# Four gate selects moved to GpSimd, softmax sums fetched as sixteen rows, and all engine orders rewritten, in a two-layer attention and LoRA-mixture kernel

## The reference

```
for attn in (a, b):
    x = x + attn(layernorm(x))          # 32 query heads, 8 key/value heads of 16, RoPE, causal softmax
    x = x + ffn(layernorm(x))
ffn(x): gate = x @ gate_w.T             # 8 experts
        two largest, softmax over the two -> w_full (8 weights, 6 of them zero)
        x @ base_w.T + base_b + 2 * sum_e w_full[e] * (x @ lora_A[e].T) @ lora_B[e].T
```

## Time and profile before

| | us |
|---|---|
| median of 3 runs | 813.37 |
| lowest, highest | 803.45, 813.75 |
| the profiled execution | 808.43 |
| its span, first to last instruction | 806.6 |
| TensorE busy | 737.9 |
| VectorE busy | 578.8 |
| GpSimd busy | 566.0 |
| ScalarE busy | 491.5 |

### The profile page before, as it was taken

How to read it: one execution, slowest core, us unless ns; L and a number is a source line. 1 busy time by engine, 2 the same in 40 slices (tenths; PEclk the granted TensorE clock), 3 DMA queues, 4 the chain that set the end, 5 groups by cost and what they waited for, 6 DMA issues and landing times.

```text
span 806.6 us, 15131 instructions
## 1 busy us (share of the span) xinstructions
PE 737.9 (91%) x4340; PEld 562.3 (70%) x4340; DVE 578.8 (72%) x2771; ACT 491.5 (61%) x1086; POOL 566.0 (70%) x669
## 2 busy tenths in 40 slices
PE   7579999999999988989998999999989999989966
PEld 6458467778777765777776787777768677756645
DVE  5587768696878959578684968778585977768333
ACT  5545666575766756567665666766565676566512
POOL 4574787768595967959688695958768596875501
PEclk9778899999999999999999999999999999999888
DMA  9623434545325265352436434253444425342010
GB/s 321 165 75 81 107 88 112 132 111 133 93 92 135 78 161 154 95 122 90 117 98 165 117 109 117 91 122 92 127 109 126 102 84 113 98 109 85 24 49 27
DMA packets 52957, 89.31 MB, mean 111 GB/s; under 512 B 16389, under 2 KB 21253, under 8 KB 52873
## 3 DMA queue, kind: packets, MB, share of 16 engines
q1 hardware_dynamic: 50568, 87.29, 40.8%
q10 hardware_dynamic: 2304, 1.05, 0.5%
HBM read 24.34 MB, written 9.44 MB: 42 GB/s over the span
## 4 chain that ended last, share of the span: by engine, by line
PE 36%; POOL 19%; DMA 19%; DVE 9%; issue 6%; ACT 5%; SPq 4%; ACTq 1%; POOLq 0%; DVEq 0%
DMA QK<-R 7%; DMA ND<-sums 6%; PE SB L444 6%; DVE tw L1031 4%; PE T L460 4%; PE SA L423 3%; POOL R L205 3%; POOL ND L230 3%; POOL PT L1130 3%; PE T L402 2%; PE SA L427 2%; POOL Qs L199 2%; PE T L403 2%; PE T L404 2%; DVE SA L968 2%
## 5 line engine op out<-in xcount | busy, mean ns | idle before, releaser
L968 DVE CUSTOM_DVE_ANT_0 SA<-SA,mask 128x128 f32<-128x128 f32 (+1 forms) x1024 | 333.6, 385 | 59.1 <-PE SA L427 46.1
L764 ACT ACTIVATE PT<-SB 128x512 f32<-128x512 f32 x384 | 218.0, 594 | 80.9 <-PE SB L444 75.8
L1130 POOL TENSOR_SCALAR_AFFINE_SELECT PT<-PT 128x512 f32<-128x512 f32 x256 | 160.3, 634 | 70.6 <-ACT PT L764 68.9
L444 PE MATMUL SB<-QK 100*128 100x512 f32 x384 | 161.5, 438 | 10.7 <-DMA QK<-mT 5.5
L968 DVE DVE_READ_ACCUMULATOR2_ANT nm<- 128x1 f32 x1024 | 141.3, 138 | 0.0
L423 PE MATMUL SA<-QK 96*128 96x512 f32 x256 | 109.2, 428 | 9.9 <-DVE nm L968 8.7
L402 PE MATMUL T<-XH,WQh 128*128 128x256 f32 x384 | 112.1, 292 | 5.0 <-DVE XL L934 4.2
L403 PE MATMUL T<-XL,WQh 128*128 128x256 f32 x384 | 110.7, 288 | 0.0
L404 PE MATMUL T<-XH,WQl 128*128 128x256 f32 x384 | 110.5, 288 | 0.0
L444 PEld LDWEIGHTS SB<-QK 100*128 100x128 f32 x384 | 74.3, 195 | 31.4 <-ACT PT L764 11.7
L460 PE MATMUL T<-PT,V 128*32 128x512 f32 x768 | 91.3, 609 | 3.9 <-DVE X L1004 1.4
(11 more groups left out here) (104 smaller groups left out, 1684.8 us busy)
## 6 DMA issues: line engine op xcount, KB each, us to landing
QK<-Rh SPq DMA_DIRECT2D x64, 256.0 KB, 4.5
QK<-R SPq DMA_DIRECT2D x64, 192.0 KB, 3.9
Qs<-Qf SPq DMA_DIRECT2D x64, 128.0 KB, 2.3
QK<-R SPq DMA_DIRECT2D x64, 128.0 KB, 2.8
ND<-sums SPq DMA_DIRECT2D x64, 128.0 KB
ND<-EF SPq DMA_DIRECT2D x32, 128.0 KB, 2.0
mid<-X SPq DMA_DIRECT2D x16, 256.0 KB, 2.8
X<-mid SPq DMA_DIRECT2D x8, 512.0 KB, 3.7
```

What stands on the lines that cost most here:

```text
L444: e.matmul(SB[k % 2][:, :].rearrange("p (j q) -> p j q", j=4), keys(p, 100)[:, u % 2, i // 2, :], queries(p, 100)[:, :, min(i, 1), :], sta ...
L764: e.activation(PT[:, k % RING, :], SB[k % 2][:, :], ACT.Exp, scale=0.25).then_inc(S["ex"], 1)
L968: ins = e.tensor_tensor_reduce(x, x, mask[:, 256 - n:256], 1.0, LOWEST, ALU.add, ALU.max, nm[:, p % 2, 0, 8 * a + 2 * h + q:8 * a + 2 * h ...
L1130: e.affine_select(out=blk, in_=blk, compare_op=ALU.is_ge, fill=0.0, base=0, pattern=[[0, 4], [1, 128]], channel_multiplier=-1).then_inc(S[ ...
```

## The change

1. `gt` runs on GpSimd, on 8 experts in place of 9 columns, directly behind `ol(2s-2)` and in front of `fH`. It is the same four `tensor_scalar` instructions.
2. `xc` copies 16 rows of sums of 1024 values in place of 8 (four copies of each head group, before two), Lc is 128 x 128 in place of 128 x 64, `sums` is 16 x 1024, and each of the two DMAs of `rr` reads 16 rows, each given to 4 partitions, in place of 8 rows given to 8.
3. The lists of all five engines are new. The number of steps of each kind stays.

```diff
-                e.dma_start(Lc[:, :], EF[1:P:16, :, :, :, :].rearrange("p o q j t -> p (o q j t)")).then_inc(S["lc"], 16)
+                e.dma_start(Lc[:, :], EF[1:P:8, :, :, :, :].rearrange("p o q j t -> p (o q j t)")).then_inc(S["lc"], 16)
...
-                e.dma_start(sums.rearrange("a (b c) -> (a b) c", c=64), Lc[:, :]).then_inc(S["rd"], 16)
+                e.dma_start(sums.rearrange("a (b c) -> (a b) c", c=128), Lc[:, :]).then_inc(S["rd"], 16)
...
-                        "r (o x) -> o r x", o=2)[o].unsqueeze(1).to_broadcast([8, 8, 512])).then_inc(S["rr"], 16)
+                        "r (o x) -> o r x", o=2)[o].unsqueeze(1).to_broadcast([16, 4, 512])).then_inc(S["rr"], 16)
...
-                        ins = e.tensor_scalar(tw[:, i, k, :, :], iota[:, :], mif[:, i, k:k + 1], wsel[:, i, k:k + 1],
+                        ins = e.tensor_scalar(tw[:, i, k, :], iota[:, :], mif[:, i, k:k + 1], wsel[:, i, k:k + 1],
```

More of the change, by code:

```diff
@@ L526, in _ @@
[L526 to L531, removed]
@@ new lines, in _ @@
+            causal(15, 2); rs_(3, 0); mu(2); ol(2); gt(0); rc(3, 2); fH(0); ra(3, 2); causal(16, 0); rc(3, 0)
+            rm(3); ra(3, 0); causal(16, 2); causal(17, 0); rc(3, 1); causal(17, 2); causal(18, 0); rs_(3, 1)
+            mu(3); causal(18, 2); rl(3, 2); ol(3); ra(3, 1); rl(3, 0); causal(19, 0); causal(19, 2); rl(3, 1)
+            causal(20, 0); causal(20, 2); power("f", 2); power("a", 10); power("a", 11); addbias(2)
+            power("f", 3); causal(21, 0); causal(21, 2); causal(22, 0); addbias(3); causal(22, 2); causal(23, 0)
@@ L1200, in _ @@
+            rs_(4, 2); causal(23, 2); mu(4); ol(4); rs_(4, 0); gt(1); rc(4, 2); fH(1); causal(24, 0); rc(4, 0)
+            ra(4, 2); causal(24, 2); rm(4); causal(25, 0); causal(25, 2); ra(4, 0); rc(4, 1); causal(26, 0)
+            mu(5); rl(4, 2); causal(26, 2); ol(5); rs_(4, 1); rl(4, 0); ra(4, 1); causal(27, 0); causal(27, 2)
+            rl(4, 1); power("f", 4); causal(28, 0); causal(28, 2); addbias(4); power("f", 5)
             for s in range(4, 12):
+                if s == 9:
+                    split_low_p(21)
+                causal(8 * s - 3, 0)
@@ new lines, in _ @@
+            mu(22); causal(95, 2); power("a", 28); ol(22); power("a", 29); rc(13, 2); gt(10); rs_(13, 0); fH(10)
+            causal(96, 0); rc(13, 0); ra(13, 2); ra(13, 0); rm(13); causal(96, 2); causal(97, 0); causal(97, 2)
+            rl(13, 2); causal(98, 0); rc(13, 1); causal(98, 2); causal(99, 0); mu(23); rs_(13, 1); ol(23)
+            ra(13, 1); rl(13, 0); causal(99, 2); rl(13, 1); power("f", 22); causal(100, 0); causal(100, 2)
+            power("a", 30); addbias(22); power("a", 31); causal(101, 0); power("f", 23); addbias(23)
@@ new lines, in _ @@
+            causal(101, 2); causal(102, 0); causal(102, 2); causal(103, 0); rs_(14, 2); causal(103, 2); mu(24)
+            ol(24); rc(14, 2); gt(11); rs_(14, 0); causal(104, 0); fH(11); rc(14, 0); ra(14, 2); ra(14, 0)
+            rm(14); causal(104, 2); causal(105, 0); rl(14, 0); rl(14, 2); causal(105, 2); mu(25); rc(14, 1)
+            ol(25); causal(106, 0); causal(106, 2); causal(107, 0); rs_(14, 1); causal(107, 2); ra(14, 1)
+            causal(108, 0); rl(14, 1); power("f", 24); causal(108, 2); addbias(24); causal(109, 0)
@@ new lines, in _ @@
+            power("f", 25); causal(109, 2); addbias(25); causal(110, 0); causal(110, 2); causal(111, 0)
+            causal(111, 2); rs_(15, 2); mu(26); ol(26); rc(15, 2); gt(12); rc(15, 0); causal(112, 0); fH(12)
+            rs_(15, 0); ra(15, 2); ra(15, 0); rm(15); causal(112, 2); causal(113, 0); causal(113, 2); rc(15, 1)
+            rl(15, 2); mu(27); rs_(15, 1); ol(27); ra(15, 1); rl(15, 0); causal(114, 0); causal(114, 2)
+            causal(115, 0); causal(115, 2); rl(15, 1); causal(116, 0); causal(116, 2); power("f", 26)
@@ L1254 @@
+            addbias(29); causal(127, 2); mu(30); ol(30); gt(14); fH(14); power("f", 30); addbias(30)
+            power("f", 31); addbias(31); gt(15); fH(15)
 _IN = ["x", "wqa", "woa", "wqb", "wob", "wg", "wb", "wl", "bias", "trig", "kmask", "krow", "iden", "mask", "iota"]
```

778 lines of the change are left out of this document (362 added, 416 removed).

## The result

The changed kernel takes 795.24 us (median of 20 runs, 788.62 to 800.74); the kernel before, timed as often, 809.3 (797.22 to 817.5). The ratio is 0.988 (95% interval 0.984 to 0.991): 7 to 13 us faster, under 2%. The profiled execution took 791.22 us against 808.43. The changed kernel, timed once more there as a yardstick, had 0.985 (0.981 to 0.989).

A forecast was written before the change was run, and what follows sets the result against it. TensorE was taken as the bound, busy 357.2 of 381.0 us in the loop. From the profiled 808.43 us, terms of -10, -4, -4.5, -2, +4 and -1 make -17.5, so 790.9, forecast as 791; range 775 to 813.

The forecast's parts named there:

- QK<-R, -10: TensorE's A(4s+4, 0), moved six steps behind PV(2s), no longer waits for a `st` DMA: 10 of 12.7 us back.
- xc 2.0: In the even halves' chain of sums after PV(2s-2), the copy xc was counted at 2.0 us.
- nm, -4: TensorE's wait for the maxima from VectorE falls by 4 of 8.7 us once gt has left VectorE.
- the clock, -4.5: Three dips of TensorE's clock in the loop, 1.5 us each, go with the waits that let it fall: 4.5 us.
- gt: Moving the selects to GpSimd takes 39.1 us off VectorE and costs GpSimd 1.0 us a slot, range 0.9 to 2.3.
- GpSimd becomes the bound: Rival, chance 0.2: gt costs 2.3 us, the fetch is no shorter, mu(2s-1) comes late; 801 us, or 805.
- Sixteen rows: Fetching the sums in sixteen rows shortens each fetch by 1 us; VectorE's reciprocal takes 0.4 us more each time.
- QK<-mT, -2: M2, mc, mr and the B behind them get 1 to 2 us more room: 2 of TensorE's 5.5 us wait go.
- +4 for GpSimd's new waits: Late ol, late fetch and the late `st` behind it on GpSimd add 4 us: 0.3 us in each of 14 slots.
- VectorE freed elsewhere, -1: A term of the sum: time freed on VectorE gives 1 us elsewhere in the run.
- Start and end, 0: Reordering at the kernel's start and end comes to 0 together, within 2 us either way.

The follow-up runs named there:

- A behind PV: The changed kernel with A(4s+4, 0) directly behind PV(2s) again in TensorE's loop body; ratio 0.984 to the kernel before, median 792.8 us.
- gt twice: The changed kernel with the four selects done twice on GpSimd, the first set into an unread buffer; ratio 1.017 to the kernel before, median 820.0 us.
- eight rows: The changed kernel with the sums fetched in eight rows as before, all else as changed; ratio 0.972 to the kernel before, median 783.7 us.
- `xl` behind `xc`: The changed kernel with only the 512 KB load xl(s+3) put behind xc(2s) in SyncE's body; ratio 0.965 to the kernel before, median 777.5 us.

## Why the prediction came out as it did

The range (775 to 813) held, the sign was right, and the profiled execution, 791.22, lies on the forecast of 791. That is partly luck. The gain was smaller than forecast: 7 to 13 us by the ratio, 14.1 between the medians of all runs, against 17.5; and the terms missed on both sides. By the steps:

- *QK<-R, -10.* The mechanism was right as far as it went (12.7 to 2.0), the gain wasn't there. "A behind PV" gives the wait back and the time stays. This is the step that failed: I priced a wait of 12.7 us at 10 by its length, and did not look what was next late at the same place. What was next was in the diff: `xc(2s)` last in SyncE's body behind a 512 KB load and a 256 KB `st`, and `rp(2s-2)` first in VectorE's. I took the 2.0 us landing of the earlier trace rows for a copy that in its new place takes 4.3 to 6.0 ("xc 2.0" in the chain of the even half).
- *nm, -4, and the clock, -4.5.* The first had the wrong sign, +7.5 us of wait, by that same copy. The second gave nothing: as many stretches of the loop at the lower clock, three of 3.4 us each, are in the trace after (at 327, 485 and 532 us) as in that of before (321, 441, 581). Those of after begin 1.0 to 1.6 us behind the ends of TensorE's three longest waits in the loop (3.5, 2.2 and 2.7 us), one for an exponential and two for the maxima.
- *gt.* 1.0 us a slot was taken; it is 1.6 (402 ns each), inside the bounds 0.9 to 2.3 and near the 1.7 that I worked out from twice VectorE's undisturbed time. In the new orders the move was worth nothing that shows: 0.4% the wrong way with the late copy, 0.6% the right way without it, both within the errors. Rival "GpSimd becomes the bound" had the mechanism right: "gt twice" pays for nearly all that is added, and in the old orders the move alone costs 1.8%. I gave it a chance of 0.2, because the path by my count had 0.4 to 1.8 us to spare; with gt at 1.6 the upper end is gone.
- *Sixteen rows.* Taken as 1 us a fetch. By the updates of its semaphore, first issue to landing, an odd fetch took 3.6 to 4.1 us before and 3.1 to 3.4 with the rows alone, an even one of the loop 6.0 and 5.2 in the mean: 0.6 to 0.8 by the rows. With the new orders an even one takes 4.5 with eight rows and 3.6 with sixteen, so what stands ahead of the fetch in the queue counts for more than its rows. GpSimd's wait fell by 33 us with the orders and by 15 without. But I valued it by the chain it lies in, not by the end of that chain. What is left of the wait does not lie at mu(2s-1), as I had it, but at even halves, nearly all outside the loop. Doubling the reciprocal was +0.4 us a step, as taken, and I hid it under the time that gt gave back; its cover wasn't there, since it stands behind the late copy.
- *QK<-mT, -2.* Gone: 5.5 us to none.
- *+4 for GpSimd's new waits.* OL of GpSimd costs TensorE 1.3 us in all, in the split body; but that body also has the longest wait, 3.5 us for an exponential. The two make 4.8 us, so the size is about right; that all of it is GpSimd's doing is argued, not shown.
- *VectorE freed elsewhere, -1.* No run shows this term: with gt back on VectorE in the new orders the time did not rise.
- *Start and end, 0.* The stretches around the loop gave 3.1 and 4.5; OL's wait at the end fell from 6.0 to 4.4. Neither was tried apart, so their causes are argued at most. Without these 7.7 us, for which I had put 0, the profiled execution would not have met 791.

In the windows of the loop, 381 and 370 us, TensorE's idle time fell by 6.1 us and its busy time by 4.9, at the same mean clock; the second is in no term of the sum. So the gain is that of the orders, as far as the runs tell: the rows gained in the old orders and cost in the new, gt showed no gain in either, and the place of one copy withheld another 2%. The new orders without both were not run, and which of their moves gives the gain is not shown.

What stays open: why eight rows gain 10.7 us (12.6 by the medians) where the waits explain 5 to 6; whether eight rows and `xl` behind `xc` add up (they act on the same wait, so not fully); why gt on VectorE turned from even to slightly worse. None of these was run.

## What to carry to other kernels

A wait that the profile shows is worth only the distance to the next thing that is late at the same place; before you count it, list what else is released there, DMAs by their new place in the queue included. The landing time of a transfer belongs to its place and not to its kind: look at which bytes are issued in the two microseconds ahead of it, and keep big loads that nobody waits for behind small copies that a chain waits for. An engine that is busy 80% of the time can have next to no slack: double its suspected step once and see what the time does.

## What the runs showed of the hardware

The same 64 KB copy over the same queue, at the same place of the loop, landed 2.0 us after its issue (one body of eight: 2.7) in the kernel with both transfers behind it, 2.0 to 3.2 with 256 KB issued 2 us ahead, and 4.3 to 6.0 with 512 and 256 KB issued 1 to 1.6 us ahead. The Trainium skill says that all DMAs of a kernel land on the same 16 engines and serialize ("SBUF — State Buffer", Can I just issue two DMAs to hit both halves?); the three ranges agree.

The select of 8 or 9 columns took VectorE a mean of 666 and 676 ns in the old order and 347 or 414 in the new one, 269 to 1846 ns for a single one, and 0.87 us for four with GpSimd idle; on GpSimd it took 386 to 407 ns in all 64 instructions of the yardstick. For a step this small GpSimd (1.54 us for four at 132.28 of the trace after) cost nearly twice what VectorE did undisturbed, less than VectorE in the old order and about as much as in the new, and its price was steady.
